# A four-layer graph network on one core: VectorE's own-part additions of the first convolution are split between ScalarE and GpSimd, and a copy of the moments is dropped

## What is computed

```python
h = relu(layernorm(x)); x = x + L0(h)    # agg(h) @ Wl.T + b + h @ Wr.T, relu
h = relu(layernorm(x)); x = x + L1(h)    # two SAGE convolutions
h = relu(layernorm(x)); x = x + L2(h)    # convolution, relu, own layernorm
h = relu(layernorm(x)); x = x + L3(h)    # two GCN convolutions
```

## Time and profile before

| | us |
|---|---|
| median of 3 runs | 668.75 (668.55 to 669.43) |
| the profiled execution, its own time | 668.7 |
| its span in the trace | 666.8 |
| PE busy | 647.4 (97%) |
| PE weight loads busy | 525.6 (79%) |
| DVE busy | 375.8 (56%) |
| ACT busy | 304.3 (46%) |
| POOL busy | 42.8 (6%) |

### The profile page before, as it was taken

One profiled execution on the slowest core, in us unless ns is written; L12 is line 12 of the kernel. 1 busy time (PEld: TensorE's weight loads), 2 busy tenths in 40 slices (PEclk: granted clock), 3 DMA queues, 4 the chain that ended last, 5 costly groups with the idle time before them and its releaser, 6 DMA issues. The chain is left out here.

```text
span 666.8 us, 11295 instructions
## 1 busy us (share of the span) xinstructions
PE 647.4 (97%) x3199; PEld 525.6 (79%) x3200; DVE 375.8 (56%) x870; ACT 304.3 (46%) x629; POOL 42.8 (6%) x45
## 2 busy tenths in 40 slices
PE   6989999999999999999999999999998899999997
PEld 4336777778888888888888888888886898899886
DVE  6998998855664433324344567554999731440222
ACT  4886777644422134752214341213676863464210
POOL 2000000000000000000000000000356070000000
PEclk9999999999999999999999999999999999999999
DMA  6311111142460002100001020000200000000102
GB/s 221 100 21 21 31 33 36 31 141 64 146 131 0 0 1 79 63 1 0 0 0 65 15 64 0 0 0 2 79 0 1 0 2 1 1 0 1 47 17 94
DMA packets 26272, 25.17 MB, mean 38 GB/s; under 512 B 14076, under 2 KB 17972, under 8 KB 26232
## 3 DMA queue, kind: packets, MB, share of 16 engines
q1 hardware_dynamic: 24952, 22.12, 11.5%
q10 hardware_dynamic: 1280, 2.56, 1.1%
HBM read 17.20 MB, written 4.20 MB: 32 GB/s over the span
## 5 line engine op out<-in xcount | busy, mean ns | idle before, releaser
L1619 PE MATMUL ps<-p_hi,cstage 128*128 128x512 f32 x400 | 156.4, 391 | 0.0
L1619 PE MATMUL ps<-p_lo,cstage 128*128 128x512 f32 x400 | 155.7, 389 | 0.0
L1525 PE MATMUL ps<-w_hi,hT_hi 128*128 128x512 f32 x320 | 128.9, 403 | 0.6 <-issue 0.3
L1525 PE MATMUL ps<-w_hi,hT_lo 128*128 128x512 f32 x320 | 125.1, 391 | 0.0
L1525 PE MATMUL ps<-w_lo,hT_hi 128*128 128x512 f32 x320 | 124.8, 390 | 0.0
L1619 PEld LDWEIGHTS ps<-p_hi,cstage 128*128 128x128 f32 x400 | 75.1, 188 | 16.5 <-issue 0.4
L1619 PEld LDWEIGHTS ps<-p_lo,cstage 128*128 128x128 f32 x400 | 75.1, 188 | 15.4
L1030 DVE TENSOR_SCALAR src_hot<-iota,nodeT 128x640 bf16<-128x640 f16 x210 | 70.8, 380 | 4.2 <-issue 2.0
L1504 PE MATMUL ps<-src_hot,dst_hot 128*128 128x320 bf16 x420 | 67.6, 306 | 5.3 <-DVE src_hot L1030 2.8
L1525 PEld LDWEIGHTS ps<-w_hi,hT_lo 128*128 128x128 f32 x320 | 60.0, 188 | 13.1
L1525 PEld LDWEIGHTS ps<-w_hi,hT_hi 128*128 128x128 f32 x320 | 60.1, 188 | 12.7 <-issue 1.1
(11 more groups left out here) (152 smaller groups left out, 904.2 us busy)
## 6 DMA issues: line engine op xcount, KB each, us to landing
x<-in_x ACTq DMA_DIRECT2D x1, 2304.0 KB
out_x<-x SPq DMA_DIRECT2D x9, 256.0 KB
wstage<-in_L_gnn_W SPq DMA_DIRECT2D x2, 1024.0 KB, 5.4
swap<-count SPq DMA_DIRECT2D x2, 800.0 KB, 8.7
count<-swap SPq DMA_DIRECT2D x2, 800.0 KB, 8.4
wstage<-in_L_gnn_W_l SPq DMA_DIRECT2D x2, 512.0 KB, 4.2
w_own<-in_L_gnn_W_r SPq DMA_DIRECT2D x1, 1024.0 KB, 11.0
vec<-in_L_gnn_b SPq DMA_DIRECT2D x4, 256.0 KB, 7.7
```

Of the source, the lines that this page charges most:

```text
L1525: last = nc.tensor.matmul(ps[:, bank, :], a[:, r, k, :], w[:, slot, k, :], start=n == 0, stop=n == len(pairs) - 1)
L1619: last = nc.tensor.matmul(ps[:, AGG + r, :], cstage[:, part, k, :], p_[:, k, :], start=n == 1, stop=n == 2 * len(parts) * NT)
```

## The change

Three edits, all in L0:

1. first_own moves from DVE to ACT and becomes a plain copy of q (PSUM to own, 128x512). In each block it stands behind phi of b-2; for tiles 8 and 9 it stands behind phi of these tiles, the last of them ahead of ACT's wait for big_ready. q_done is now given by ACT.
2. POOL adds the bias row to own in SBUF, tile by tile, in a loop ahead of its branch on big_i, and counts own_biased. DVE's receive of tile i waits for own_biased of i+1, and SP's reload of the bias slot waits for all ten.
3. In this stage bn_aggr writes into one of two slots of mv_first, which ACT and DVE read, so the copy into mv (line 1011) is gone. bn_stats of tile i waits for mv_done of i. The later layers keep the three instructions.

```diff
+    mv_first, _ = place("mv_first", [P, 2, 2], F32)
...
                         sp.wait_ge(q_done, tile(after, NT - 1))
+                        if after == L0:
+                            sp.wait_ge(own_biased, NT)
...
+                if s == L0:
+
+                    pool.wait_ge(vec_loaded[VSLOT[L0]], VCOUNT[L0])
+                    with pool.Fori(0, NT) as i:
+                        pool.wait_ge(q_done, tile(L0, i))
+                        nc.gpsimd.tensor_tensor(own[:, bass.ds(i, 1), :], own[:, bass.ds(i, 1), :],
+                                                vec[:, VSLOT[L0]:VSLOT[L0] + 1, :], ALU.add).then_inc(own_biased, 1)
...
+            def first_own(i):
+
+                act.wait_ge(q_ready, tile(L0, i))
+                nc.scalar.copy(own[:, bass.ds(i, 1), :], ps[:, q_bank(L0, 0):q_bank(L0, 0) + 1, :]).then_inc(q_done, 1)
...
-                deviation(0, b)
+                first_deviation(b, r)
                 counts_of(b - 1, 1)
                 found = visits_of(act, visited, b, 1)
                 phi(L0, b - 2, r)
+                first_own(b - 2)
                 receivers(b, 1, found)
...
             phi(L0, NT - 2, 0)
+            first_own(NT - 2)
...
             phi(L0, NT - 1, 1)
+            first_own(NT - 1)
...
+            def first_statistics(i):
+                dve.wait_ge(mv_done, i)
+                dve.sem_inc(passed_dve, 1)
+                nc.vector.bn_stats(stats[:, :], x[:, bass.ds(i, 1), :]).then_inc(stats_done, 1)
+
+            def first_moments(i, r):
+                dve.wait_ge(stats_done, i + 1)
+                dve.sem_inc(passed_dve, 1)
+                nc.vector.bn_aggr(mv_first[:, r, :], stats[:, :]).then_inc(mv_done, 1)
...
-            def first_own(i):
-
-                dve.wait_ge(q_ready, tile(L0, i))
-                nc.vector.tensor_tensor(own[:, bass.ds(i, 1), :], ps[:, q_bank(L0, 0), :], vec[:, VSLOT[L0], :],
-                                        ALU.add).then_inc(q_done, 1)
...
                 p_rest(L0, b - 2, r)
-                first_own(b - 2)
                 givers(b, 1, found)
...
-                statistics_1(0, b + 1)
+                first_statistics(b + 1)
                 found = visits_of(dve, visited, b + 1, 0)
-                statistics_2(0, b + 1)
-                statistics_3(0, b + 1)
+                first_moments(b + 1, 1 - r)
                 lo(L0, b, r)
...
                     dve.wait_ge(q_done, tile(s, i))
+                    if s == L0:
+                        dve.wait_ge(own_biased, i + 1)
```

More of the change, by code:

```diff
@@ L237, in gnn_kernel @@
         sem("hidden_done"), sem("u_pads"), sem("biased"), sem("span_coarse"), sem("span_exact"))
+    own_biased = sem("own_biased")
     passed_dve, passed_pool = sem("passed_dve"), sem("passed_pool")
@@ L621, in deviation, with first_deviation @@
                                      bias=eps[:, 0:1]).then_inc(std_done, 1)
+            def first_deviation(i, r):
+                act.wait_ge(mv_done, i + 1)
+                nc.scalar.activation(std[:, bass.ds(i, 1)], mv_first[:, r, 1:2], ACT.Sqrt,
+                                     bias=eps[:, 0:1]).then_inc(std_done, 1)
+            def first_own(i):
+                act.wait_ge(q_ready, tile(L0, i))
+                nc.scalar.copy(own[:, bass.ds(i, 1), :], ps[:, q_bank(L0, 0):q_bank(L0, 0) + 1, :]).then_inc(q_done, 1)
             visited = [act.alloc_register(f"act_visited{h}") for h in range(2)]
@@ L695, in _ @@
             receivers(1, 0, found)
-            deviation(0, 0)
+            first_deviation(0, 0)
             counts_of(0, 1)
@@ L700, in _ @@
             split_first(1, range(2, KF))
-            deviation(0, 1)
+            first_deviation(1, 1)
             counts_of(1, 0)
@@ L1009, in statistics_3 @@
             def statistics_3(v, i):
-                dve.wait_ge(aggr_done, NT * v + i + 1)
+                dve.wait_ge(aggr_done, NT * (v - 1) + i + 1)
                 nc.vector.tensor_scalar(mv[:, bass.ds(i, 1), :], mv_now[:, :].unsqueeze(1), 1.0, None,
                                         ALU.mult).then_inc(mv_done, 1)
+            def first_statistics(i):
[6 more added lines that the diff above has]
+                nc.vector.bn_aggr(mv_first[:, r, :], stats[:, :]).then_inc(mv_done, 1)
             visited = [dve.alloc_register(f"dve_visited{h}") for h in range(2)]
@@ L1052, in features @@
                         dve.wait_ge(x_done, NT * NEW_X[s - 1] + i + 1)
-                    nc.vector.tensor_scalar(z[:, r, :], x[:, bass.ds(i, 1), :], mv[:, bass.ds(i, 1), 0:1],
+                    mean = mv_first[:, r, 0:1] if s == L0 else mv[:, bass.ds(i, 1), 0:1]
+                    nc.vector.tensor_scalar(z[:, r, :], x[:, bass.ds(i, 1), :], mean,
                                             rstd[:, bass.ds(i, 1)], ALU.subtract, ALU.mult).then_inc(z_ready, 1)
@@ L1101, in _ @@
             dve.wait_ge(x_loaded, 32)
-            statistics_1(0, 0)
+            first_statistics(0)
             found = visits_of(dve, visited, 1, 0)
-            statistics_2(0, 0)
-            statistics_3(0, 0)
+            first_moments(0, 0)
             split_first(1, range(0, 2))
@@ L1108, in _ @@
             features(L0, 0, 0)
-            statistics_1(0, 1)
+            first_statistics(1)
             found = visits_of(dve, visited, 1, 1)
-            statistics_2(0, 1)
-            statistics_3(0, 1)
+            first_moments(1, 1)
             givers(1, 1, found)
@@ L1116, in _ @@
             features(L0, 1, 1)
-            statistics_1(0, 2)
+            first_statistics(2)
             found = visits_of(dve, visited, 2, 0)
-            statistics_2(0, 2)
-            statistics_3(0, 2)
+            first_moments(2, 0)
             lo(L0, 1, 1)
             givers(2, 0, found)
-            dve.wait_ge(vec_loaded[VSLOT[L0]], VCOUNT[L0])
             def merged(b, r):
@@ L1166, in _ @@
             nc.vector.reciprocal(dis[:, :], dis2[:, :]).then_inc(scale_step, 1)
-            first_own(NT - 2)
             dve.wait_ge(scale_step, 2)
@@ L1174, in _ @@
             p_rest(L0, NT - 1, 1)
-            first_own(NT - 1)
             dve.wait_ge(scale_step, 3)
```

## The result

The changed kernel takes 670.54 us in the median of 22 executions (669.11 to 674.03); the kernel before, beside it, 668.71 (22 executions, 667.35 to 669.76). The ratio is 1.0033, with a 95% interval of 1.0022 to 1.0044: slower by some 2 us. The forecast was 670.6, in a range of 669.5 to 672.0.

A forecast was written before the change was run, and what follows sets the result against it. PE was taken to bound the kernel from 50 us on, DVE from 30 to 50 us. From 668.7 us, less 0.4 for the moments' copy, plus 2.3 for the last copy, other terms 0: 670.6 us, range 669.5 to 672.0.

The forecast's parts named there:

- The bound of each stretch: DVE sets the pace from 30 to 50 us, PE from 50 to 137 us and behind 150 us.
- The rival of a VectorE that paces the blocks: Between 50 and 137 us, DVE's freed 7.8 us come off the time, giving 662.8 us; chance 0.07.
- The moments' copy: Before 50 us, dropping the copies of tiles 0 and 1 gains 0.4 us, bounds 0 to 1.0.
- ACT's eight copies: Inside the blocks, ACT's added copies of 0.60 us each cost 0, at most 4.8 us without cover.
- The last copy: Ahead of the first aggregation, ACT's copy for tile 9 delays stage(0); PE stands empty 2.3 us, bounds 2.1 to 2.9.
- POOL on DVE: Behind the stage, POOL's additions lengthen four w_lo by 1.3 to 4.6 us; at most 1.3 reaches PE, 671.9; chance 0.10.
- the slack: In the aggregation, 3.3 us between receive(0)'s end at 154.87 and PE asking for it at 158.2.
- The two terms: The early gain of 0.4 us before 50 us and the 2.3 us loss ahead of the first aggregation.
- the handover: From q of tile 9 to the first aggregation, PE empty for 2.3 us, because ACT's copy precedes stage(0).

The follow-up runs named there:

- best16: The changed kernel with ACT's copy of tile 9 behind the stage casts, POOL's additions behind DVE's w_lo, and a 16-bit table of windows: 668.02 us.
- moments16: The kernel before with only the moments' copy dropped and the table of windows held as 16-bit numbers: 668.28 us.
- base16: The kernel before with the table of windows held as 16-bit numbers, no asserted bound: 668.52 us.
- moments: The kernel before with only the moments' copy dropped, plus an asserted bound on each load of window numbers: 668.22 us.
- ownlate: The changed kernel with the asserted bound on window loads, and ACT's copy of own of tile 9 behind its two first stage casts: 669.40 us.
- loadfirst: The changed kernel with the asserted bound on window loads, and ACT's load of big_i ahead of its last copy: 670.26 us.
- holdstage: The kernel before with the asserted bound on window loads, and ACT waiting for q of tile 9 ahead of big_ready, without copying: 671.95 us.
- again: The changed kernel with an asserted bound on each load of window numbers: 670.91 us.
- base: The kernel before with only an asserted bound added on each loaded pair of window numbers: 669.81 us.

## Why the prediction was right, and where it was not

**The bound of each stretch** held. PE set the pace from 50 us on; 7.2 us of DVE work went and PE's busy time stayed at 86.6 of 87 us. The rival of a VectorE that paces the blocks is refuted for this kernel: best16, with own on ACT, and moments16, with own on DVE, take 99.03 and 99.06 us from p of tile 0 to the aggregation. It is nearer than the forecast made it, though: base16 and the kernel before, which do all of DVE's work, take 99.19 and 99.32, up to 0.3 us more. With the bound, moments takes 99.16 and ownlate 98.63: a few register instructions more on every engine and DVE's freed time is worth half a us.

**The moments' copy** was put at 0.4 us and gave 0.39 to 0.44 in like pairs (21.63 to 21.24, 21.56 to 21.14, 21.55 to 21.11).

**ACT's eight copies** in the blocks cost nothing, as forecast: the stretch got no longer.

**The last copy** was put at 2.3 us and measured 2.28, with PE idle for 2.31 us. The 0.80 us from the copy's start to the cast was 0.77, and loadfirst shows that the register work waits for the copy's dispatch and then runs beside it. One reading in this term was right by luck. The forecast took the 0.25 us between the first cast's end and PE's start in the kernel before for a delay of PE; but there PE was busy with q until then, so the row shows no such delay. There is one of the same size: with PE idle, it starts 0.24 us behind the cast in the changed kernel, in loadfirst and in holdstage (149.50 - 149.26, 150.18 - 149.94, 151.47 - 151.23). Of the Trainium skill's description (Perfetto Trace Analysis, section on DVE / Act engine instructions), by which the sequencer goes on past a waiting instruction, the changed kernel's load of big_i and loadfirst show the opposite for register work behind a waiting instruction in this queue.

**POOL on DVE** was there and its size was right (3.3 us on w_lo, forecast 1.3 to 4.6), but the slack was mis-sized. The forecast took receive's end, 154.87, for when DVE was ready, and forgot that DVE had itself waited 0.96 us for PE there; and it looked only at t_done. The way by which POOL reaches PE first is another one, shown by ownlate: moments, ACT's deviation, and the cast queued behind it. In the changed kernel this missed PE by half a us, because PE was late itself. The Trainium skill (SBUF — State Buffer, section "Who interferes with whom") fits the w_lo: 2.50 us alone, 5.79 and 6.40 beside POOL, 2.50 again once POOL waits. The same section has the one-input moments' copy hit too if it runs in a 2-port mode, and it was, at 1.10 us.

**What the sum left out** is the clock behind the hole. In 9 of the 22 executions of the changed kernel the mean clock is 0.992 to 0.995 and the time 671.5 to 674.0 us; in the 13 of 0.997 it is 669.1 to 671.6. holdstage and loadfirst caught the fall behind the hole in their profiles, at 1.5 and 1.6 us; in the changed kernel's own profile and in again's it did not fall there. That the slower nine are executions with such a fall is the likely reading, but it is not shown: their profiles weren't taken, and a mean clock doesn't say where it was lost. The profiles with one recorded fall have 0.997, that of the changed kernel among them, whose fall lies at 517 us in the third layer; those with two, or one of twice the length, have 0.994 or 0.995, and base16 and best16 have that without any hole ahead of the aggregation.

So the median agrees with 670.6 more closely than its parts deserve. The two terms give 668.7 + 2.3 - 0.4. The 13 executions with a mean clock of 0.997 have a median of 669.45, only 0.7 us over the kernel before; the nine with less have 672.3, and the median of all falls between the two. By places, the profiled execution differs from that of the kernel before by -1.15 us at the end of the first count, -0.44 to p of tile 0 and +1.99 to the aggregation (101.31 - 99.32: the hole, less 0.3 us of gain in the blocks, which the forecast put at 0). The first of these is what no term covered. By the spacing of its matmuls it comes of the clock and not of the change, and in the twelve profiles it makes up to 1.8 us between one first count and another. Part of the agreement is therefore luck; the handover and the two copies are not.

## What to carry to other kernels

A copy that nobody waits for can still cost its whole wait if it stands in an engine's queue ahead of something that was early: here a copy of 0.6 us emptied PE for 2.3 us, since the work behind it had been done while PE was still busy. Put such a copy behind the work that the busiest engine will ask for next; and when a hole is closed, look at what it had hidden, since here POOL's additions cost 0.84 us as soon as PE was on time.

## What was not expected of the hardware

- TensorE's granted clock fell to 0.50 behind a hole of 2.0 to 2.2 us in two of four profiles with such a hole (holdstage and loadfirst; not in the changed kernel's and again's), and cost 1.5 to 1.6 us of a full PE. None of the eight profiles without the hole has it there. Every one of the twelve profiles has another hole of 2.3 us, between 513 and 520 us in the third layer, and behind it the clock fell in eight, not in before, moments, moments16 and holdstage. There PE waits for others anyway: from the transposes at 190 us to the end of the span these eight take 476.8 to 477.7 us and the four without the fall 476.8 to 477.3.
- The small copy of the moments, 128x2, took 1.10 us on DVE beside POOL's additions, in place of 0.17.
- The asserted bound on 20 loads per engine cost base some 0.3 us between p of tile 0 and the aggregation, in one profile of each.
- The first count takes 13.55 to 15.33 us with nothing in the program to account for it. It follows how many of its matmuls, behind 1.4 to 2.4 us in which PE stood idle, start every 0.27 us in place of 0.14: none in the changed kernel's profile, 12 to 23 in the other eleven. What decides the number stays open.
